# Attention and expert routing on one core: last matrix split moved, second PSUM bank for two transposes, experts chosen in batches of 16, 8 and 8

## What is computed

```python
h = layernorm(x) * (1 + ca) + sa
x = x + ga * attention(h)          # q, k = relu(...), scan over time with decay gamma, num / denom
h = layernorm(x) * (1 + cb) + sb
logits = h @ Wr.T + br             # 8 experts
expert = argmax(logits)            # one expert for each of the 4096 rows
x = x + gb * (relu(h @ W1[expert].T + b1[expert]) @ W2[expert].T + b2[expert])
```

## Time and profile before

| What | Value |
|---|---|
| Median of 3 runs | 524.05 (522.47 to 524.83) |
| The profiled execution | 522.32 |
| Its span | 520.4, 15203 instructions |
| Mean granted TensorE clock | 0.942 of full speed |
| Busy: TensorE / VectorE / ScalarE / GpSimd | 459.6 (88%) / 399.6 (77%) / 326.3 (63%) / 289.9 (56%) |

### The profile page before, as it was taken

The page is one execution under the profiler, slowest core; times in us unless marked ns, Lnnn a source line. Parts: engine busy times, 40 slices in busy tenths (PEclk is TensorE's granted clock), DMA queues, the critical chain, the costliest instruction groups (busy, mean ns, idle before and its releaser), DMA issues.

```text
span 520.4 us, 15203 instructions
## 1 busy us (share of the span) xinstructions
PE 459.6 (88%) x4392; PEld 407.3 (78%) x4393; DVE 399.6 (77%) x1061; ACT 326.3 (63%) x863; POOL 289.9 (56%) x463
## 2 busy tenths in 40 slices
PE   5899999999998999996415999999999999999980
PEld 3599888888886888885214998898898889888970
DVE  2769998888988899888583788777777877777750
ACT  2437677766676667763333777677767776777650
POOL 2327677777775677656223256555655565556531
PEclk9979999999999999997556999999999999999996
DMA  8654444433434443311002112211222122111000
GB/s 295 247 182 144 143 139 122 122 119 116 140 130 131 142 142 119 116 42 52 10 1 83 33 45 80 58 63 56 61 75 61 46 64 68 54 53 50 28 7 0
DMA packets 23968, 47.37 MB, mean 91 GB/s; under 512 B 4719, under 2 KB 17650, under 8 KB 21752
## 3 DMA queue, kind: packets, MB, share of 16 engines
q1 hardware_dynamic: 17976, 32.74, 19.0%
q0 software_dynamic: 4992, 12.60, 8.0%
q10 hardware_dynamic: 960, 1.57, 0.9%
HBM read 36.13 MB, written 13.51 MB: 95 GB/s over the span
## 4 chain that ended last, share of the span: by engine, by line
PE 39%; issue 26%; POOL 19%; DVE 9%; POOLq 3%; DMA 1%; ACT 0%; ACTq 0%; DVEq 0%
PE ps_qk L1083 10%; POOL out_rows L498 8%; POOL arena L478 5%; PE ps_va L1089 5%; PE ps_kv L1043 5%; PE ps_o L1035 5%; POOL arena L492 4%; PE ps_va L1071 3%; PE ps_o L1031 3%; PE ps_h L1098 3%; POOLq L490 2%; PE ps_h L1050 2%; POOL arena L485 2%; PE ps_k L1058 2%; PE ps_x L1107 1%
## 5 line engine op out<-in xcount | busy, mean ns | idle before, releaser
L1171 PE MATMUL ps_o<-w,arena 128*128 x936 | 108.7, 273 | 2.3 <-DVE arena L995 1.6
L1171 PEld LDWEIGHTS ps_o<-w,arena 128*128 128x128 f16 x936 | 89.9, 98 | 14.7 <-issue 4.0
L965 DVE COPY w<-w 128x2048 f16 x78 | 61.6, 790 | 29.8 <-issue 24.2
L599 ACT ACTIVATE arena<-ps_qk,arena 128x128 f32<-128x128 f32 x156 | 44.5, 368 | 58.5 <-PE ps_qk L1151 58.5
L478 POOL TENSOR_TENSOR arena<-arena 128x256 f32<-128x256 f32 x39 | 28.1, 721 | 70.9 <-DVE arena L999 70.9
L1083 PE MATMUL ps_qk<-arena,wqkv_sb 128*128 128x128 f32 x512 | 64.5, 281 | 0.0
L1151 PE MATMUL ps_qk<-arena,w 128*128 128x128 f16 x936 | 60.2, 222 | 4.9 <-DVE arena L982 4.4
L1151 PEld LDWEIGHTS ps_qk<-arena,w 128*128 128x128 f16 x936 | 53.7, 99 | 13.1 <-issue 8.3
L1083 PEld LDWEIGHTS ps_qk<-arena,wqkv_sb 128*128 128x128 f32 x512 | 61.8, 197 | 0.9 <-DMA bqk_sb<-in_bqk 0.9
L485 POOL DMA_INDIRECT arena<-token_rows,slot_token x39 | 42.0, 1077 | 35.1 <-POOL arena L478 28.4
L1151 PE MATMUL ps_va<-arena,w 128*128 128x128 f16 x936 | 59.3, 220 | 0.0
(11 more groups left out here) (165 smaller groups left out, 920.9 us busy)
## 6 DMA issues: line engine op xcount, KB each, us to landing
w<-in_w_raw SPq DMA_DIRECT2D x16, 1024.0 KB, 5.3
token_rows<-arena SPq DMA_DIRECT2D x64, 128.0 KB, 1.9
arena<-in_x SPq DMA_DIRECT2D x32, 128.0 KB, 2.1
b_sb<-in_b2b SPq DMA_DIRECT2D x1, 1024.0 KB, 5.1
w<-in_wmod ACTq DMA_DIRECT2D x1, 768.0 KB, 9.2
wqkv_sb<-in_wqkv SPq DMA_DIRECT2D x1, 768.0 KB, 8.4
mod_rows_sb<-mod_rows SPq DMA_DIRECT2D x1, 768.0 KB, 4.9
arena<-token_rows,slot_token POOLq DMA_INDIRECT x39
```

The source lines that it names most:

```text
L599: last = act.activation(hid[:, f, :], bank[("qk", "va")[h]][:, (f % 4) * P:(f % 4 + 1) * P], ACT.Relu, bias=consts_now[:, r, f:f + 1], sca ...
L965: dve.tensor_copy(now[:, :, i * F // 2:(i + 1) * F // 2], of[:, :, i * F // 2:(i + 1) * F // 2]).then_inc(s_w1, 1)
L1171: last = pe.matmul(bank["o"][:, 0:D], hid_parts[:, r % 2, b, f, :], w[:, bass.ds(m + 1, 1), a, f * D:(f + 1) * D].rearrange("p a d -> p (a ...
```

## The change

It has three parts. The last matrix (m = 15) is left out of the slots: ScalarE makes its four first-part pieces right after its last attention slot, before it waits for the routing, and VectorE makes the four second-part pieces after it has signalled `s_routed`, before the first copy of W1, with a wait for their completion. Chunk 30 uses bank x in place of bank h for its transposes and logits, and the transposes of chunks 30 and 31 wait for the logits of one chunk earlier than before. `choose` runs for chunks 0 to 15, 16 to 23 (ahead of the logits of chunk 24, in slot (14,1)) and, after the last slot, 24 to 31.

```diff
@@ -301,6 +301,10 @@
 
         block = ctx.enter_context(nc.Block())
 
+        def wide_bank(n):
+
+            return bank["x" if isinstance(n, int) and n == NCH - 2 else "h"]
+
         def att_item(k, u, lag):
             return item(k, u, lag, B, NCH)
 
@@ -511,9 +515,11 @@
                 act.dma_start(wmod_sb[:, :, a:b], wmod[:, :, a:b]).then_inc(s_cmod[i], 16)
             act.wait_ge(s_c, 16)
             act.activation(c_exp, c_sb, ACT.Exp, scale=-1.0).then_inc(s_cexp, 1)
-            def hi_piece(k, u, j):
+            def hi_piece(k, u, j, last=False):
 
                 if (m := matrix_at(k, HI + 1 - u)) is not None:
+                    if isinstance(m, int) and (m == NM - 1) != last:
+                        return
                     i = 2 * (1 - u) + j
                     if i == 0:
                         act.wait_ge(s_wscale, m + 1)
@@ -554,7 +560,7 @@
                     n, g, r = it
                     act.wait_ge(s_h2x, n + 1)
                     need(act, s_lg, n - 1)
-                    act.activation(h2_t[:, r], bank["h"][:, 0:D].rearrange("p (k t) -> p k t", k=DK),
+                    act.activation(h2_t[:, r], wide_bank(n)[:, 0:D].rearrange("p (k t) -> p k t", k=DK),
                                    ACT.Copy).then_inc(s_h2t, 1)
                 hi_piece(k, u, 0)
                 if it := att_item(k, u, XPOSE):
@@ -577,6 +583,10 @@
                 hi_piece(k, u, 1)
 
             slots(act, *ATT, slot)
+
+            for k, u in ((NM, 1), (NM + 1, 0)):
+                for j in range(2):
+                    hi_piece(k, u, j, last=True)
 
 
             act.wait_ge(s_minus, 1)
@@ -752,9 +762,9 @@
                     dve.wait_ge(s_wmaxh, m + 1)
                     dve.tensor_reduce(lane_max, piece_max, AX_X, ALU.max).then_inc(s_wboth, 1)
 
-            def lo_piece(k, u, j):
-
-                if (m := matrix_at(k, LO)) is None:
+            def lo_piece(k, u, j, last=False):
+
+                if (m := matrix_at(k, LO)) is None or (m == NM - 1) != last:
                     return
                 i = 2 * u + j
                 dve.wait_ge(s_whi, PIECES * m + i + 1)
@@ -835,10 +845,10 @@
                     dve.bn_aggr(mv2[:, r, :], st2[:, r, :]).then_inc(s_mv2, 1)
                 if it := att_item(k, u, LOGIT):
                     n, g, r = it
-                    if n in (16, 28):
-                        choose({16: 0, 28: 16}[n], n)
+                    if n in (16, 24):
+                        choose(n - 16 if n == 16 else 16, n)
                     dve.wait_ge(s_lg, n + 1)
-                    dve.tensor_tensor(logits[:, n, :], bank["h"][:, D:D + NE], br_sb[:], ALU.add).then_inc(s_lgr, 1)
+                    dve.tensor_tensor(logits[:, n, :], wide_bank(n)[:, D:D + NE], br_sb[:], ALU.add).then_inc(s_lgr, 1)
                 if it := att_item(k, u, PROJ):
                     n, g, r = it
                     dve.wait_ge(s_vp, n + 1)
@@ -886,7 +896,7 @@
             tile_f = scratch[:, 2016:2016 + NT]
             token_f = scratch[:, 2056:2056 + NT]
 
-            choose(28, NCH).then_inc(s_chosen, 1)
+            choose(24, NCH).then_inc(s_chosen, 1)
             for b in range(B):
                 dve.wait_ge(s_sx[b], 16 * (NCH // B))
                 dve.wait_ge(s_sh[b], 16 * (NCH // B))
@@ -943,6 +953,11 @@
             dve.tensor_copy(slot_token[:], token_f).then_inc(s_tokens, 1)
             dve.tensor_scalar(slot_late[:], token_f, float(S), None, ALU.is_ge)
             dve.tensor_scalar(slot_early[:], token_f, float(S), None, ALU.is_lt).then_inc(s_routed, 1)
+
+            for u in range(2):
+                for j in range(2):
+                    lo_piece(NM + 1, u, j, last=True)
+            dve.wait_ge(s_wlo, NM)
 
             dve.wait_ge(s_idx, 1)
             dve.wait_ge(s_b2, 16)
@@ -1047,7 +1062,7 @@
                     n, g, r = it
                     pe.wait_ge(s_h2t, n + 1)
                     for h in range(DK):
-                        last = pe.matmul(bank["h"][:, D:D + NE], h2_t[:, r, h, :], wr_sb[:, h, :],
+                        last = pe.matmul(wide_bank(n)[:, D:D + NE], h2_t[:, r, h, :], wr_sb[:, h, :],
                                          start=(h == 0), stop=(h == DK - 1))
                     last.then_inc(s_lg, 1)
                 if it := att_item(k, u, SCORE):
@@ -1093,9 +1108,9 @@
                     n, g, r = it
                     pe.wait_ge(s_h2, n + 1)
                     need(pe, s_h2t, n)
-                    need(pe, s_lgr, n)
+                    need(pe, s_lgr, n - 1 if isinstance(n, int) and n >= NCH - 2 else n)
                     for h in range(DK):
-                        last = pe.transpose(bank["h"][:, h * P:(h + 1) * P], h2[:, r, h * P:(h + 1) * P], ident)
+                        last = pe.transpose(wide_bank(n)[:, h * P:(h + 1) * P], h2[:, r, h * P:(h + 1) * P], ident)
                     last.then_inc(s_h2x, 1)
                 if it := att_item(k, u, XPOSE):
                     n, g, r = it
```

## The result

The changed kernel takes 518.80 in the median of 12 runs (515.65 to 520.21); the kernel before, on the same chip, 522.27 (519.78 to 524.83). The ratio is 0.9932, 95% interval 0.9912 to 0.9952: 3.5 faster (2.5 to 4.6), or 0.68%. The forecast was 1.2 faster and within 0.5%. The profiled execution after took 520.21 with a span of 517.7; its granted clock was 0.953 against 0.942.

A forecast was written before the change was run, and what follows sets the result against it. TensorE was taken as the limit mid-attention, single waits through ScalarE and VectorE at attention's end. -2.5 + 1.9 - 0.6 = -1.2 took the median from 524.05 to 522.8, with 8 in 10 between 520.8 and 525.6.

The forecast's parts named there:

- The choice in slot (14,1): cost 1.9: Mid-attention, the choice of 8 chunks makes TensorE wait, with no idle time to give it back: +1.9.
- The clock falls: Rival: after the new pause in slot (14,1) TensorE's clock falls, costing about 1.7, time 524.5; chance 0.33.
- The step that bounded a fall between pauses of 1.62 and 2.29: The clock fell after 2.29 but not after 1.62; where between them it sets in decides for the new 1.9.
- End of attention: gain 2.5: Last chunks: chunk 31's L841 at 252.26 against 254.90, 2.64 gained, less 0.1 for the longer last choice: about -2.5.
- The chunk of 2.15: End of attention: with the second bank one chunk takes 0.70 + 0.43 + 1.02, in place of the ring of 2.50.
- the last choice: After the last slot: growing from 4 chunks to 8 costs 0.1 or less.
- the second bank does nothing: Rival, end of attention: h2 comes late anyway, a chunk still takes 2.5, 2 x 0.37 lost, 523.5; chance 0.07.
- The first gather: gain 0.6: Feed-forward start: first gather falls from 1.73 to 1.05, 0.7 earlier; copies meeting later gathers leave -0.6.
- VectorE late: Rival, feed-forward start: copies wait for gathers' ends, L982 starts 0.7 later instead of 0.6 earlier, 524.1; chance 0.10.
- VectorE's and ScalarE's pieces at nothing: After the slots and the routing: ScalarE's four (2.9) and VectorE's four (3.0) fit in idle time, costing about nothing.

The follow-up runs named there:

- e6: Changed kernel with the choice of chunks 16 to 23 spread one instruction per slot over slots (14,1) to (16,1): 519.52, 0.9946 of the kernel before.
- e5: The changed kernel as it is, measured and profiled a second time: 519.41, 0.9946 of the kernel before.
- f1: Kernel before plus moved pieces and second bank, batches 16, 12, 4, with a useless extra choice of chunks 16 to 23 in slot (14,1): 519.85, 0.9931.
- f3: Kernel before plus moved pieces and second bank, batches 16, 12, 4, without extra choice: 520.41, 0.9947 of the kernel before.
- e3: Kernel before with only the batches of the choice changed to 16, 8, 8: 521.71, 0.9986 of the kernel before.
- e1: Kernel before with only the last matrix's pieces moved, bank and batches as before: 521.15, 0.9973 of the kernel before.
- e8: Changed kernel with VectorE waiting for the first gather's rows before its four last-matrix pieces: 522.9 in its one run.
- g1: Kernel before with the four second-part pieces of the last matrix made a second time after the routing: 521.41, 0.9998 of the kernel before.
- e9: Changed kernel with VectorE reading chunk 27's logits before waiting for the last scores in slot (16,0): 517.69, 0.9915 of the kernel before.
- e11: Changed kernel with chunk 27's logits read early and the choices of chunks 0 to 15 and 16 to 23 spread over slots: 514.72, 0.9863.
- g2: The kernel before, unchanged, measured for a second profile: 1.0002 of the kernel before.

## Why the prediction was wrong

- **The base.** The forecast of 522.8 started from a median of three runs, 524.05. Twelve runs gave 522.27. This is 1.8 of the 4.0 between 522.8 and 518.8. It is not the whole reason that the measured time lies below the range: moved down by 1.8 the range would begin at 519.0, still 0.2 above 518.8. The other 2.3 is the change itself, forecast at -1.2 and measured at -3.5.
- **"The choice in slot (14,1): cost 1.9. Nothing hides it ... TensorE has no idle time to give it back"** is the step that failed. The pause was sized well (1.82) and the clock did not fall after it, as forecast. But the cost is not the pause alone. It shifts the next pause, of 2.33 in slot (16,0), and after the shift the clock stays up through the work behind that pause, or falls only 1.3 to 1.4 into it. The profiles give 1.0 back in slots (16,*). In whole times e6 against e5 says that all of it comes back, give or take 1.2, and f1 against f3 agrees within a wider 2; how the other 0.8 would come back is open. The row of 2.33 stood in the trace of before, with a fall of the clock 1.3 behind it, and I passed it by, because its wait is the same with and without the change:

```profile
240.29 0.41 PE L1098 MATMUL ps_h<-cst,arena 128*128 128x128 f32 x2 [2.33 <-DVE logits L841]
```

```profile
240.30:241.60 1.30, 1.30 (x7) 1.19 (x8) 0.94 (x5) 0.87 (x2) 1.12 (x3) 1.00 0.19 65
241.60:244.90 3.30, 3.00 (x10) 2.42 (x8) 2.56 (x8) 1.23 (x3) 1.97 (x3) 0.51 0.05 17
```

- **"The clock falls", the rival at 0.33,** looked for the fall behind the new pause. There was none at 1.82, in seven profiles. The clock did matter, at another place and with the other sign. The step that bounded a fall between pauses of 1.62 and 2.29 took the length of the pause as what decides; pauses of 2.30 and 2.33 were followed by a fall in some profiles and not in others.
- **End of attention: gain 2.5.** From chunk 31 to tile 0 the two profiles after show -2.97 and -2.99, of which the gather is 0.2: 2.8 against 2.5. The chunk of 2.15 was 1.91 and 2.02, since the next transposes began 0.87 after the start of L1065 and not 1.02; the last choice cost 0.27 and not 0.1. By parts: batches 1.42 (e3), split 0.59 (e1), bank nothing alone and 1.1 beside the split. The rival "the second bank does nothing" is out for the full change, though true of the bank alone (its 2 x 0.37 should read 2 x 0.35, from 2.50 and 2.15; its time of 523.5 stands).
- **The first gather: gain 0.6** was 0.2. The step read a row of 0.69 as blocked time because it equalled the copy's length; e8 shows that the first gather is longer than the others by itself, and that a two-input instruction over a gather costs 0.3, against what the step took from the earlier trace rows. "VectorE late" did not happen: the idle time before L997 was 0.69, and both copies took 0.69. The exclusive lock that the Trainium skill describes (SBUF — State Buffer, section Who interferes with whom) would have held the copy of 274.71, begun inside the third gather, until that gather's end at 275.70; it took its 0.69. No run here shows a full block of a copy by a gather.
- **VectorE's and ScalarE's pieces at nothing** was right: L528 ends at 254.05, before the routing begins at 254.45, and VectorE still has 0.69 to spare before L997.
- **Left over.** The segments of the two profiles after against the two of before sum to +1.82 - 0.69 - 2.93 - 0.37 (tiles 0 to 10) - 0.42 (tiles 10 to 38) = -2.6, against 3.5 (2.5 to 4.6) measured. The feed-forward phase's 0.8 was in no step of the prediction; half of it comes with the four VectorE instructions (g1), and the difference at tile 10, -0.2 to -0.9 in the two profiles after, also varies between profiles of one kernel. The 0.9 that no segment holds lies within the scatter of the measurement and of the profiles. Both stay open, so the account explains the direction and most of the size, not all of it.

## What to carry to other kernels

A pause of TensorE has two prices: its length, and what it does to the clock at the next pause. Before charging the first in full, look for later pauses in the same stretch that are long enough for the clock to fall behind them (here 2.33, while 1.82 was not), take them away first if that is cheap (here one moved read: e9 against e5, 1.7 in the medians, the intervals overlapping), and then spread the work that makes the earlier ones: e11, with both, took 514.72 against 522.29, 0.9863 [0.9838, 0.9888], faster than the kernel before and the changed kernel. And take more than one profile of the kernel before where the clock falls near the change: here a single one hid 1.05.

## What the runs showed of the hardware

- After the pause of 1.82 the clock stayed at 1.00 in all seven profiles that have it. The pause of 2.30 in slot (10,1) was followed by 0.50 in 8 of 18 profiles. The pause of 2.33 in slot (16,0) was followed by a fall at once in some (e6, g2), 1.3 later in others (before, e5), and by none for over 5 in three (the changed kernel, e3, e8).
- A pause with no purpose, 1.82 long, left the time where it was within 2 (f1 against f3), and taking such a pause away made no difference either (0.1, give or take 1.2; e6 against e5), in a stretch where TensorE is fully busy.
- The first indirect gather of GpSimd took 1.26 with no VectorE piece or copy over it, 1.56 under two-input instructions, 1.73 under a copy; later ones 1.05 in the median, and the fourth 1.36 where the two-input instructions lay over it (e8).
